# Unnormalised keys in a delta-rule layer: norms moved into other factors, a transposition dropped, convolution taps planned one by one

## The reference

```python
qkv = causal_conv(x @ W_qkv.T, conv_w)           # 4 taps per channel
q, kk, v = ...                                   # 16 heads of keys, 128 channels; 2 value heads each
kk = kk / max(norm(kk), 1e-12)
beta, decay = sigmoid(x @ W_b.T), exp(-dt * exp(A_log))
# for each token t, for each of 2 sequences and 16 x 2 heads
Sk    = k_t @ S
delta = (v_t - Sk) * beta_t
S     = S * decay_t + outer(k_t, delta)
o     = q_t @ S
out   = rmsnorm(o) * silu(z);  y = out @ W_out.T
```

## Time and profile before

| | |
|---|---|
| runs, us | 1396.16, 1393.04, 1392.79 (median 1393.04) |
| the profiled execution's own time, us | 1396.62 |
| its span, first to last instruction, us | 1394.9 |
| mean granted TensorE clock | 0.979 |
| busy share of the span | PE 94%, PEld 78%, DVE 80%, ACT 68%, POOL 61% |
| instructions | 33366 |

### The profile page before, as it was taken

The page is one execution under the profiler, slowest core; times in us unless marked ns, Lnnn a source line. Parts: engine busy times, 40 slices in busy tenths (PEclk is TensorE's granted clock), DMA queues, the critical chain, the costliest instruction groups (busy, mean ns, idle before and its releaser), DMA issues. The chain is left out here.

```text
span 1394.9 us, 33366 instructions
## 1 busy us (share of the span) xinstructions
PE 1317.5 (94%) x12564; PEld 1086.2 (78%) x12564; DVE 1119.6 (80%) x2294; ACT 946.3 (68%) x2605; POOL 847.0 (61%) x966
## 2 busy tenths in 40 slices
PE   6999999878999999999999999999999999999985
PEld 3554445667898989898888888889888888888884
DVE  4495646898989888979788988878888878887875
ACT  3105574467787878777877777868777777777664
POOL 8011124338866777576767677577776867676652
PEclk9998999989999999999999999999999999999997
DMA  9910001213111121121121111121112222113011
GB/s 323 167 32 2 5 1 46 77 42 99 39 28 43 35 87 42 28 80 36 39 74 40 41 31 41 43 69 53 27 47 62 62 62 54 55 51 88 17 54 38
DMA packets 61592, 78.84 MB, mean 57 GB/s; under 512 B 6232, under 2 KB 48856, under 8 KB 61432
## 3 DMA queue, kind: packets, MB, share of 16 engines
q1 hardware_dynamic: 56696, 62.41, 17.2%
q0 software_dynamic: 4736, 14.29, 3.7%
HBM read 63.97 MB, written 12.71 MB: 55 GB/s over the span
## 5 line engine op out<-in xcount | busy, mean ns | idle before, releaser
L2029 ACT ACTIVATE XY<-ps 128x512 f16<-128x512 f32 x384 | 219.3, 597 | 64.7 <-PE ps L1274 56.8
L1777 DVE TENSOR_TENSOR ZL<-ps,cst 128x256 f16<-128x256 f32 x384 | 152.3, 415 | 32.3 <-PE ps L1261 27.6
L1687 DVE SCALAR_TENSOR_TENSOR yv<-ps,cw,yv 128x511 f32<-128x511 f32 (+2 forms) x192 | 143.3, 746 | 14.9 <-ACT yv L1966 10.0
L973 PE MATMUL ps<-XH,WVh 128*128 128x256 f32 (+1 forms) x384 | 133.1, 347 | 0.9 <-ACT De L2053 0.8
L973 PE MATMUL ps<-XH,WVl 128*128 128x256 f32 (+1 forms) x384 | 122.5, 319 | 0.0
L973 PE MATMUL ps<-XL,WVh 128*128 128x256 f32 (+1 forms) x384 | 122.5, 319 | 0.0
L2062 ACT ACTIVATE sq<-O 128x128 bf16<-128x128 f32 x256 | 79.4, 310 | 58.5 <-DVE O L1836 21.6
L1271 PE MATMUL ps<-ZL,XY 128*128 128x64 f16 x1536 | 105.2, 193 | 3.4 <-DVE ZL L1777 2.1
L1261 PE MATMUL ps<-XY,LT 128*128 128x64 f16 x1536 | 97.9, 193 | 9.0 <-ACT XY L2029 6.1
L1271 PEld LDWEIGHTS ps<-ZL,XY 128*128 128x128 f16 x1536 | 77.6, 98 | 34.1 <-issue 16.7
L1274 PE MATMUL ps<-XY,ZL 128*128 128x64 f16 x1536 | 104.0, 193 | 0.0
(11 more groups left out here) (313 smaller groups left out, 4505.4 us busy)
## 6 DMA issues: line engine op xcount, KB each, us to landing
RC<-crow SPq DMA_DIRECT2D x128, 128.0 KB
WV<-in_WV SPq DMA_DIRECT2D x16, 512.0 KB, 3.6
WK<-in_WK SPq DMA_DIRECT2D x16, 256.0 KB, 2.7
WO<-in_WO SPq DMA_DIRECT2D x16, 256.0 KB, 2.7
rows_out<-st SPq DMA_DIRECT2D x7, 512.0 KB
KS<-spread SPq DMA_DIRECT2D x12, 256.0 KB, 13.7
QS<-spread SPq DMA_DIRECT2D x12, 256.0 KB, 19.3
w<-in_w SPq DMA_DIRECT2D x4, 512.0 KB, 8.7
```

The costliest lines, as they stand in the source:

```text
L973: m = pe.matmul(o, a, b, start=c + k == 0, stop=c == 1 and k == 2)
L1687: m = dve.scalar_tensor_tensor(out=dst[:, k:512], in0=ps[:, bk, 0:512 - k], scalar=cw[:, h, j, 3 - k:4 - k], in1=dst[:, k:512], op0=ALU.mu ...
L1777: leave(dve.tensor_tensor(half(ZL[:, k - 2], k, 0), p, lv(k), ALU.mult), "a", u, k)
L2029: leave(act.activation(changed(u, k), ps[:, bank("b", u, k), :].rearrange("p (c n t) -> p c n t", c=2, t=1 << (k - 1)), ACT.Copy), "b", u, k)
```

## The change

Keys stay as the convolution leaves them. `K` (three heads deep, in place of `yk` and `KT`) is the convolution's output, channel x token, and is used directly by `gram` and `KS`. `KN` is its transposition, copied without a scale by one ACT instruction per half. The norms go elsewhere: both decay products of a chunk get 1/norm² as a per-partition scalar (one DVE instruction per half in place of one for both), the state scale `bE` is multiplied by 1/norm² by POOL, and the values are multiplied by the norm when ACT writes them (two instructions of 128x256 for one of 128x512). POOL's part `kn` has five instructions for two. The turn back `KT` is gone, on PE and on ACT. The three taps of a convolution are three parts of the plan (`ck1`, `ck2`, `ck3`, ...), which other DVE parts may stand between; before, they were one. RANK and LATER have new values throughout, several planned costs are changed, and a part that follows one of its own engine is planned 0.08 us after it. So the order of every engine, and the banks, are new, in layer 0 too, where no instruction changes.

```diff
-    "KS": {"ACT": -200.58, "DVE": 11.77, "PE": -1.09}, "KT": {"ACT": 16.77, "PE": -28.02},
...
+    "KS": {"ACT": -35.71, "DVE": 41.66, "PE": -8.88}, "U": {"ACT": 137.37, "PE": -118.07},
...
-                key = int((at + p.later) * (1 / self.GRAIN)), p.rank
+                key = int((at + p.later) * (1 / self.GRAIN)), p.rank, p.no
...
-                q.due = max(q.due, end + self.DELAY[p.eng])
+                q.due = max(q.due, end + (0.08 if q.eng == p.eng else self.DELAY[p.eng]))
...
+def plan_taps(P, x, rank):
+    for k in (1, 2, 3):
+        P.add(tap(k, x), rank, ("DVE", 0.66, (x, "ACT") if k == 1 else (tap(k - 1, x), "DVE")), gives=x if k == 3 else None)
...
-                  ("ACT", 1.62, (("kn", h - 1, b), "POOL") if h else None),
-                  ("POOL", 1.25, (("kns", h - 1, b), "ACT") if h else None), takes=True)
-        P.add(("kns", h, b), rank[5 + 2 * b], ("ACT", 1.0, (("kn", h, b), "POOL"), old), gives=("kn", h, b))
-    for b in range(2):
-        P.add(("KT", h, b), rank[8 + b], ("PE", 0.44, (("kns", h, b), "ACT")), ("ACT", 0.49, old), takes=True,
-              gives=("KT", h, b))
+        P.add(("kn", h, b), rank[4 + 2 * b], ("PE", 0.44, (("ck3", h, b), "DVE")),
+              ("ACT", 1.47, (("kn", h - 1, b), "POOL") if h else None),
+              ("POOL", 1.9, old, (("pre", 5), "DVE")), takes=True)
+        P.add(("kns", h, b), rank[5 + 2 * b], ("ACT", 0.49, (("kn", h, b), "ACT"), old), gives=("kn", h, b))
...
-                  ("ACT", 0.49, to), takes=True, gives=x)
+                  ("ACT", 0.74, to, (("kn", h, b), "POOL")), takes=True, gives=x)
...
-    keys = [(("KT", h, b), "ACT") for b in range(2)] + [(("cq", h, b), "DVE") for b in range(2)]
+    keys = [((what, h, b), "DVE") for what in ("ck3", "cq3") for b in range(2)]
...
-          ("DVE", 0.6, (("dec", u), "ACT"), earlier(2, "py", "POOL")), takes=True)
+          ("DVE", 0.7, (("dec", u), "ACT"), *[(("kn", h, b), "POOL") for b in range(2)], earlier(2, "py", "POOL")), takes=True)
...
+                    if k == 1:
+                        w.wait_ge(d_l1, 64)
+                        w.wait_ge(s_raw, nth("ACT", *x))
+                    else:
+                        w.wait_ge(s_tap[k - 1], nth("DVE", *tap(k - 1, x)))
...
+                    for b in range(2):
+                        w.wait_ge(s_rn, nth("POOL", "kn", u // 4, b))
+
+                    def masked(to, k, decay):
+                        for b in range(2):
+                            n = 4 * b + u % 4
+                            m = dve.scalar_tensor_tensor(out=v22(to)[:, b], in0=both(k)[:, b],
+                                                         scalar=k_inv2[:, u // 4 % 3, n:n + 1], in1=v22(decay)[:, b],
+                                                         op0=ALU.mult, op1=ALU.mult)
+                        return m
...
+                    leave(act.activation(KN[:, h % 3, 4 * b:4 * b + 4, :], q4(bank("kn", h, b)), ACT.Copy), "kn", h, b)
...
+                    w.wait_ge(s_rn, nth("POOL", "kn", h, b))
+                    for k in range(2):
+                        n = 4 * b + 2 * q + k
+                        m = act.activation(V[:, n, :], ps[:, bank(*x), 256 * k:256 * k + 256], ACT.Copy,
+                                           scale=k_norm[:, h % 3, n:n + 1])
...
-                    pool.tensor_tensor(rb, ss[:, 4 * b:4 * b + 4], mh[:, 0:4], ALU.pow).then_inc(s_rk, 1)
+                    pool.tensor_scalar(q, ss[:, four], 1.0, 1e-24, ALU.mult, ALU.max).then_inc(s_rk, 1)
+                    w.wait_ge(s_rk, at - 3)
+                    pool.tensor_tensor(r, q, mh[:, 0:4], ALU.pow).then_inc(s_rk, 1)
+                    w.wait_ge(s_rk, at - 2)
+                    pool.tensor_tensor(rr, r, r, ALU.mult).then_inc(s_rk, 1)
+                    pool.tensor_tensor(nk, q, r, ALU.mult).then_inc(s_rk, 1)
                     w.wait_ge(s_rk, at)
-                    pool.tensor_scalar(rb, rb, 1e12, None, ALU.min).then_inc(s_rn, 1)
+                    w.wait_ge(s_dd, 13)
+                    pool.tensor_tensor(be, be, rr.unsqueeze(2).broadcast_to((128, 4, 2)), ALU.mult).then_inc(s_rn, 1)
```

More of the change, by code:

```diff
@@ L64 @@
 RANK = {
[4 rows of a table removed]
[L69 to L92, removed]
[3 rows of a table added]
+    "c": {"DVE": 48.53, "PE": -22.19}, "cb": {"DMA": -91.43, "DVE": 94.64, "POOL": 118.87}, "cc": {"POOL": 165.79},
[4 rows of a table added]
+    "cv3": {"DVE": -23.94}, "dec": {"ACT": -128.31, "POOL": -48.22}, "dn": {"DVE": 113.73, "PE": -86.21},
@@ new lines @@
+    "exd": {"DVE": -260.04, "PE": -45.05}, "exg": {"ACT": -108.33, "PE": 4.86}, "exv": {"DVE": -44.71, "PE": 10.89},
+    "fWK": {"POOL": 8.05, "SP": -102.38}, "fWO": {"POOL": -95.78, "SP": 98.07}, "fWV": {"POOL": 92.58, "SP": 6.05},
+    "fin": {"DVE": -113.78, "SP": -118.07}, "fld": {"SP": -97.52}, "fs": {"ACT": 184.69}, "fst": {"SP": 83.6},
+    "fup": {"POOL": 65.29, "SP": 98.62}, "g0": {"ACT": -26.26}, "gg": {"DVE": 35.25, "PE": -116.99},
+    "gram": {"DVE": 87.86, "PE": -1.57}, "gt": {"ACT": 67.6, "PE": -22.76},
@@ L93 @@
+    "xr": {"SP": -125.99}, "xs": {"SP": -40}, "y": {"DVE": -61.07, "PE": -10.97},
 }
 LATER = {
[L97 to L105, removed]
+    "KS": {"ACT": 0.17}, "Zt": {"ACT": 0.08}, "am": {"POOL": 0.1}, "cb": {"POOL": 0.54}, "cc": {"POOL": 2.56},
@@ L106 @@
+    "sc": {"ACT": 0.35}, "sd": {"DVE": 0.69}, "spg": {"POOL": 2.37}, "sr": {"POOL": 0.23}, "stack": {"SP": 1.87},
+    "sw": {"DMA": 0.55, "POOL": 0.22}, "tn": {"DVE": 0.25}, "tn0": {"DVE": 0.36}, "top": {"ACT": 0.24},
+    "tp": {"DVE": 0.29}, "up": {"ACT": 0.59}, "xb": {"SP": 0.3}, "xs": {"SP": 0.24},
 }
@@ L231, in plan_softmax0 @@
         P.add(("mk", *x), rank, ("POOL", 0.65, (("sc", *x, 0), "ACT"), (("sc", *x, 1), "ACT")))
-        P.add(("pv", *x), rank, ("PE", 0.87 * part + 0.13, (("mk", *x), "POOL"), last and (last, "PE")), takes=j == 0)
+        P.add(("pv", *x), rank, ("PE", 0.95 * part + 0.18, (("mk", *x), "POOL"), last and (last, "PE")), takes=j == 0)
         if j == 3:
@@ L245, in plan_rows0 @@
     for b in range(2):
-        P.add(("nrm", b), -90 + 60 * b, ("DVE", 2.0, *[(("op", n), "DVE") for n in range(4 * b, 4 * b + 4)],
+        P.add(("nrm", b), -90 + 60 * b, ("DVE", 1.75, *[(("op", n), "DVE") for n in range(4 * b, 4 * b + 4)],
                                          (("nr2", 0), "DVE") if b else None), ("POOL", 1.3))
@@ L318, in plan_values @@
         x = "cv", h, v, b
-        P.add(x, rank[k], ("PE", 1.48, wv, *(ready(b) if h < 2 else ())), ("ACT", 0.58, (("Vt", h - 1, b, 1), "PE") if h else None), ("DVE", 1.99),
-              takes=True, gives=x)
+        P.add(x, rank[k], ("PE", 1.48, wv, *(ready(b) if h < 2 else ())), ("ACT", 0.58, (("Vt", h - 1, b, 1), "PE") if h else None),
+              takes=True)
+        plan_taps(P, x, rank[k])
     for q in range(2):
@@ L1762, in run_vector @@
                             w.wait_ge(*full("so", u - 4, 1))
-                        leave(dve.tensor_tensor(v22(PT[:, u % 4]), both(1), v22(E[:, :, 1:129]), ALU.mult), "gram", u)
+                        leave(masked(PT[:, u % 4], 1, E[:, :, 1:129]), "gram", u)
                 elif what == "x1":
@@ L1959, in run_scalar @@
                     w.wait_ge(*full(*x))
-                    if what == "ck" and h:
-                        w.wait_ge(*full("kn", h - 1, b))
-                    elif what == "cq" and h > 2:
+                    if what != "cv" and h > 2:
                         w.wait_ge(*full("y", 4 * (h - 3) + 3))
```

132 lines of the change are left out of this document (65 added, 67 removed), and 12 rows, old and new, of the table RANK.

## The result

The changed kernel takes **1400.68 us** (median of 5, 1399.74 to 1403.92) where the kernel before takes 1392.79 on the same chip (5 runs, 1391.83 to 1396.16): ratio **1.0055**, 95% interval 1.0037 to 1.0074. It is slower by half a per cent, outside the range of the prediction and against its sign. The profiled execution took 1402.02 us, its span is 1400.3 (before: 1396.62 and 1394.9).

What follows compares the result with a forecast made beforehand. PE was taken to bound the kernel from 300 to 1350 us. Terms -14.5 (turn back), -0.5 (waits) and -2 (order) sum to -17.0: 1379.6 us from the profiled 1396.6, 1376.0 for the median, range 1360 to 1394.

Steps and rivals of the forecast that it cites:

- The order anew: All queues and banks, SP's and POOL's included: new order takes up some of PE's idle time, -2 us.
- The work by itself: PE loses 14.5 us of key transpositions; the other engines' changes are hidden or even out and cost nothing.
- The -0.5 for the shorter way to a head's first product: Waits: gram no longer waits for KN and KT, first gram of layer 1 moves up; -0.5 us (0 to -3).
- The turn back: PE: 32 groups of 4 key transpositions go, -14.5 us, bounds 13.4 and 20.4.
- PE at 97% without one dominant wait: Support for the forecast case (1368 to 1387 us, chance 0.53): PE bounds 300 to 1350 us, so less PE work shortens it.
- The decay products: DVE: gram and pt each become two scaled halves, 0.74 us for 0.60, +17.9 us (+7.7 to +23).
- The taps: DVE convolution: other work between single taps saves up to 38 us, half taken, -19; little effect on PE's waits.
- The third case: Rival, DVE takes the place: taps not separable, DVE's 18 us come in full; 1390 to 1397 us, chance 0.14.
- POOL, +29, hidden: POOL norm part kn: three more instructions at 0.3 us, +29 us, hidden by 307 us of POOL idle time.
- ACT, -20: ACT: KT writes -15.4, kns -16.6, Vt +11.5; some 20 us lighter, costed at nothing in time.
- Slower: DVE stops for POOL at each head: Rival: masked gram product waits for POOL's norms, stopping DVE's queue, 2.4 us in 16 heads, +38; 1414 us, chance 0.12.
- PE's idle time in the long stretch moved by over 10 us: Sign the prediction is wrong: PE's idle time from 300 us to the end's last 45 us, 31.8 before in 300 to 1350.

Runs made afterwards that it cites:

- e17: The changed kernel, nothing altered, as control on the same chip as e18: 1384.09 us, ratio 1.0043 to the kernel before.
- e18: The changed kernel in its own order with three buffers for the decay row instead of two: 1354.06 us, ratio 0.9819 to the kernel before.
- e5: The new work in the kernel before's order and banks, taps in a row, keys four deep, two row buffers: 1389.67 us, ratio 1.0087 to the kernel before.
- e7: e5 with three buffers for the decay row instead of two: 1385.61 us, ratio 1.0069 to the kernel before.
- e6: The kernel before, order unchanged, with three buffers for the decay row instead of two: 1372.08 us, ratio 0.9966.
- e10: e9 with the values written unscaled in one write and two POOL norm instructions per half head instead of five: 1368.04 us, ratio 0.9929.
- e3: The changed kernel in its order, but each tile's three taps in a row where the first stood: 1443.86 us, ratio 1.0458 to the kernel before.
- e9: e7 with each masked product whole again, without the factor 1/norm^2 and its wait: 1373.88 us, ratio 0.9972 to the kernel before.
- e2: The kernel before's work, with the turn back of the keys, in the changed kernel's order and banks: 1531.41 us, ratio 1.1089.
- e14: The kernel before with the row's transfer costed at 5.0 us in its plan, not 2.5, and planned anew: 1389.18 us, ratio 1.0000.
- e12: The changed kernel, two row buffers, the row's transfer costed at 5.0 us in the plan, not 2.5, planned anew: 1362.98 us, ratio 0.9876.

## Why the prediction was wrong

By its own steps:

- **"The order anew ... I take -2, because a lighter ACT and finer DVE parts leave it more freedom."** This is the step that failed in the changed kernel: with the row in time and all else as it stands, it is at 0.9819, past the 0.988 that the prediction asked for. Its bounds were taken from PE's idle time alone; SP's queue, whose DMAs the step itself says are moved, was never priced. The prediction put the whole step at -2 us. The wait of 20.8 us for the row and the plan's 2.5 us for a transfer that takes 5.1 could both be read before. In the new order a row that is late holds up POOL in 49 places, and that costs 30.0 us of the time (e17 to e18). In the old order the same two buffers cost 4 to 5 us (e5 to e7, and 0.34% for e6).
- **The work by itself, -14.5 with everything else at nothing.** This failed too. In the old order the new work costs 12 us (e5) where the forecast has it gain 14.5; the items below say which parts. (The -0.5 for the shorter way to a head's first product was not tested.) So the forecast had three errors of like size: the work some 26 us dearer than foretold, the order with the single taps some 32 us better, and the late row some 26 us worse. That the sum missed by no more is the middle one cancelling one of the others.
- **The turn back, -14.5.** As busy time about right: 20.0 us less in the profiled execution, of which 5.6 are the first 250 us and their clock, and 9.6 in the old order (1309.3 in e6, 1299.7 in e10). As time, mis-sized: it gives about 5 us there (1 to 9 by the intervals). "PE at 97% without one dominant wait" did not mean that time taken off PE comes off the end: of the busy time that left, the stretch gave 6 us back as idle time (23.3 in e6, 29.6 in e10).
- **The decay products, DVE +17.9, "with the taps DVE ends where it was".** Mis-sized: in the timeline below a pair has a pitch of 0.78 us, not 0.74, which is +23 us against 0.60 before, the prediction's upper bound. DVE's busy time ended 12.7 us higher and not where it was. Alone it costs 13 us in the old order, where nothing pays it back. The third case had the mechanism (chance 0.14) and a size of 12 to 18 us.
- **The taps, -19.** Right in kind and near in size. e3 against the kernel after gives 17.6 us of busy time. But the prediction called what they do for PE's waits "little", from a wait of 2.4 us, and joined again they make PE wait 31.4 us for one DVE step alone.
- **POOL, +29, hidden.** The products take 0.20 to 0.22 us each, not 0.3, so +18.7. Not quite hidden: with ACT's halved write it is 5.8 us (e10 to e9).
- **ACT, -20.** 18.6 less busy.
- **Slower: DVE stops for POOL at each head.** Slower it was, but not so: what the masked product on DVE waits for in the kernel after is PE, 5.7 us in 9 places (group row below has the time), and no row names POOL. Its price was also misread: 34.2 us in 14 waits holds the one of 12.5, so the others are 1.7 us each and not 2.4.

Pitches of DVE in the kernel after, timeline, and one row of its groups by line and form:

```profile
501.50 0.74 DVE L1692 SCALAR_TENSOR_TENSOR K<-ps,cw,K 128x511 f32<-128x511 f32 x1
502.16 0.60 DVE L1826 SCALAR_TENSOR_TENSOR RH<-ps,dec,V 128x128 f32<-128x128 f32 x2
...
510.25 1.52 DVE L1692 SCALAR_TENSOR_TENSOR K<-ps,cw,K 128x511 f32<-128x511 f32 x2
511.69 0.74 DVE L1692 SCALAR_TENSOR_TENSOR QC<-ps,cw,QC 128x511 f32<-128x511 f32 x1
...
517.63 0.87 DVE L1767 SCALAR_TENSOR_TENSOR M<-ps,small,E 128x256 f32<-128x256 f32 x2
518.41 0.87 DVE L1767 SCALAR_TENSOR_TENSOR PT<-ps,small,E 128x256 f32<-128x256 f32 x2
...
L1767 DVE SCALAR_TENSOR_TENSOR M<-ps,small,E 128x256 f32<-128x256 f32 x128 | 55.5, 475 | 6.0 <-PE ps L1245 5.7
```

A tap with other work behind it has a pitch of 0.66 us (501.50 to 502.16); two taps of one tile in a row take 1.44 (510.25 to 511.69), so the second's wait for the first costs 0.12. The Trainium skill, "VectorE: DVE Perf Modes", section "The DRAIN you can't avoid", says that a chain with a semaphore behind each operation takes as long as one without. By that rule 384 taps would have saved nothing. For taps that wait for one another the trace doesn't agree: here setting them apart saved 17.6 us of busy time.

The sum as the runs have it, on the scale of about 1377 us: the new work in the old order, with two rows, +12 us (1.0087); the new order, which has the single taps apart, another 34 us less where the row is in time (1.0069 in e7, 0.9819 in e18); and the late row some 26 us more of it than in the old order (30.0 less 4.1). 12 - 34 + 26 is +4, beside a measured +6 to +8. By this sum the new order with its late row gives some 8 us net, not far from the -2 foretold, which is luck: both halves of it are over ten times as large. With the row in time the change takes 0.9795 to 0.9819 of the kernel before, and 1.5 to 1.7% less than the kernel before with the same third buffer (0.9966). The late row took that away.

By these runs the gain comes with the order and the single taps, and not with the unnormalised keys alone. Whether the kernel before would gain as much from the new ranks and planner rules and single taps of its own, without the unnormalised keys, was not tested: e2 has no room for its work, and e14 changes one cost alone.

The prediction said it would be wrong if PE's idle time in the long stretch moved by over 10 us. It moved by 20.9, and that is where it was. On the third chip the same changed kernel is idle 37.0 us there (e17) and not 52.7, so a part of the figure belongs to the chip of the result.

## What to carry to other kernels

A planner's costs are part of the kernel: when a change makes the order anew, take from the trace the real time of every transfer and compare it with the cost in the plan before trusting "the order stays as good", the queues that no edit touches above all. A wait reaches the bounding engine under another name, so a change of order is judged by the waits of *all* engines, and a third buffer for the late transfer is a small test of it that leaves the order alone. Work added to the second engine in a chain of dependences can cost over half its length (13 of 21 us here, in the old order) even when the first is 96% busy and the second 88%. And when work and order change together, each is tested by itself: here they moved the time by +12 and -34 us, which the total doesn't show.

## What the runs showed of the hardware

- From the issue of the row's two DMAs (128 KB each) to the first use it is 5.1 us (521.31 to 526.45), and by the kernel's own semaphores the issue comes after the buffer is free. A third buffer took the wait from 86.7 to 13.4 us (e17, e18), the measured cost in the plan to 33.5 (e12).
- A product of 128x4 on POOL takes 0.20 us and a power of the same shape 1.04, in the kernel after's groups by line:

```profile
L2226 POOL TENSOR_TENSOR small<-small 128x4 f32<-128x4 f32 x32 | 33.1, 1035 | 2.7
...
L2229 POOL TENSOR_TENSOR small<-small 128x4 f32<-128x4 f32 x32 | 6.4, 201 | 0.0
```

- Chips and sessions differ more than most edits here: the kernel before has medians of 1376.06, 1376.97, 1380.48, 1381.18, 1389.89 and 1392.79 us (the second and third on one chip, in two sessions). The traces of the two slowest sessions have short waits whose releaser the profile can't name, and the others have none. Two such rows of the kernel after, on the chip of the result, from the waits of the whole span:

```profile
DVE ZL L1793 <- remote: 7.3, 2, 4.1
ACT XY L2036 <- remote: 6.5, 6, 1.5
```

  The changed kernel's ratio is 1.0055 with such waits and 1.0043 without, so its own verdict doesn't hang on it; what those waits are was not found.
